# First FFN: the last two batches as tiles of chosen rows, two chains in the opening, and the choice of keys beside the tiles

## The reference, cut to what matters

```
x = x + haar_mixing(ln(x))     # q, v products, Haar transform, weights, inverse, W_out
x = x + ffn(ln(x))             # first FFN
x = x + sparse_attention(ln(x))# 16 heads: band of 128, 64 global keys, top 128 keys by a score
x = x + ffn(ln(x))             # second FFN, same weights

def ffn(x):                    # 8 experts, 128 -> 256 -> 128
    p = softmax(x @ Wg)
    w, i = top_k(p, 2);  w = w / (sum(w) + 1e-8)
    y[e] = square(relu(x @ W1[e])) @ W2[e]
    return sum over the two chosen e of w[e] * y[e]
```

## Time and profile before

| | |
|---|---|
| median of 3 runs | 570.01 us (569.81 to 571.88) |
| profiled execution, span | 568.3 us |
| PE busy | 517.5 us, 91% |
| DVE busy | 408.2 us, 72% |
| ACT busy | 350.6 us, 62% |
| POOL busy | 271.3 us, 48% |
| chain that ended last | PE 54%, DVE 30%, issue 8%, POOL 3%, ACT 3%, DMA 1% |

### The profile page before, as it was taken

One profiled execution on the slowest core, in us unless ns is written; L12 is line 12 of the kernel. 1 busy time (PEld: TensorE's weight loads), 2 busy tenths in 40 slices (PEclk: granted clock), 3 DMA queues, 4 the chain that ended last, 5 costly groups with the idle time before them and its releaser, 6 DMA issues.

```text
span 568.3 us, 13254 instructions
## 1 busy us (share of the span) xinstructions
PE 517.5 (91%) x4483; PEld 321.2 (57%) x4483; DVE 408.2 (72%) x1458; ACT 350.6 (62%) x775; POOL 271.3 (48%) x429
## 2 busy tenths in 40 slices
PE   5899999999996889988898999999998999889996
PEld 2467776767772445444544554555545553567875
DVE  2447575698999799999967878778688795134335
ACT  5476656656640266656774677676765657667763
POOL 2402030160605994674408985859916346264540
PEclk9999999999996899999999999999999999999999
DMA  7990000000000000000000000000100011575606
GB/s 228 336 273 2 0 2 1 0 2 1 11 2 13 2 15 12 8 12 16 12 14 4 15 13 13 6 20 30 34 5 13 17 42 43 196 258 173 206 19 186
DMA packets 33443, 31.99 MB, mean 56 GB/s; under 512 B 7250, under 2 KB 28502, under 8 KB 33376
## 3 DMA queue, kind: packets, MB, share of 16 engines
q1 hardware_dynamic: 31616, 27.80, 16.2%
q0 software_dynamic: 1760, 3.35, 1.7%
HBM read 8.57 MB, written 12.00 MB: 36 GB/s over the span
## 4 chain that ended last, share of the span: by engine, by line
PE 54%; DVE 30%; issue 8%; POOL 3%; ACT 3%; DMA 1%; SPq 0%; DVEq 0%; POOLq 0%; ACTq 0%
PE BANK L1565 6%; PE BANK L1547 6%; DVE QST L1221 5%; PE BANK L1615 4%; PE BANK L1665 4%; PE BANK L1640 3%; PE BANK L1668 3%; DVE SW L1175 3%; PE BANK L1501 2%; PE BANK L1511 2%; PE BANK L1671 2%; DVE X L1157 2%; DVE QST L1224 2%; DVE M L1173 2%; PE BANK L1526 2%
## 5 line engine op out<-in xcount | busy, mean ns | idle before, releaser
L819 ACT ACTIVATE PT<-BANK 128x256 f32<-128x256 f32 (+2 forms) x352 | 159.1, 492 | 98.0 <-PE BANK L1640 74.6
L553 POOL TENSOR_SCALAR OH<-IOTA,POS 128x128 bf16<-128x128 bf16 x240 | 139.8, 617 | 1.4 <-DVE POS L1189 1.0
L1216 DVE CUSTOM_DVE_ANT_0 XN_a<-BANK,BANDQ 128x256 f32<-128x256 f32 (+1 forms) x128 | 62.5, 488 | 22.9 <-PE BANK L1615 20.1
L1565 PEld LDWEIGHTS BANK<-W,PT 128*128 128x128 f32 x512 | 62.0, 192 | 15.2 <-issue 14.4
L1216 DVE CUSTOM_DVE_ANT_0 XN_c<-BANK,BANDQ 128x384 f32<-128x384 f32 (+1 forms) x128 | 62.3, 487 | 9.0 <-PE BANK L1615 7.4
L1565 PE MATMUL BANK<-W,PT 128*128 128x128 f32 x512 | 62.5, 275 | 0.0
L1547 PE MATMUL BANK<-XNT_ALL,W 128*128 128x512 f32 x128 | 60.6, 597 | 0.0
L730 ACT ACTIVATE PT<-BANK 128x512 f32<-128x512 f32 x64 | 38.0, 597 | 31.4 <-PE BANK L1547 30.9
L560 POOL TENSOR_TENSOR SUM<-NRM 128x128 f32<-128x128 f32 x16 | 7.3, 457 | 104.6 <-DVE NRM L1237 104.6
L1665 PE MATMUL BANK<-PT,V 128*32 128x256 f32 (+1 forms) x512 | 47.7, 444 | 1.9 <-ACT OS L828 0.4
L582 POOL DMA_INDIRECT yt<-QKV,IDY x31 | 30.4, 980 | 27.4 <-DVE QKV L1074 22.7
(11 more groups left out here) (300 smaller groups left out, 1185.2 us busy)
## 6 DMA issues: line engine op xcount, KB each, us to landing
xs<-W SPq DMA_DIRECT2D x1, 6984.0 KB, 27.5
KZB<-W SPq DMA_DIRECT2D x16, 256.0 KB, 2.4
KZC<-W SPq DMA_DIRECT2D x15, 256.0 KB, 2.6
QKV<-xs SPq DMA_DIRECT2D x31, 72.0 KB, 2.0
W<-w SPq DMA_DIRECT2D x2, 1024.0 KB, 8.1
X<-x SPq DMA_DIRECT2D x4, 256.0 KB, 3.2
out<-X SPq DMA_DIRECT2D x4, 256.0 KB, 2.2
KZB<-KALL SPq DMA_DIRECT2D x20, 36.0 KB, 1.9
```

The source lines that it names most:

```text
L553: last = nc.gpsimd.tensor_scalar(OH[g % 2][:, i, t, :], IOTA[:, :], POS[:, t, c:c + 1], None, ALU.is_equal)
L819: nc.scalar.activation(PT[u % PT_RING][:, 0:w], P2_BANK[u % SCORE_RING][:, 0:w], ACT.Exp, scale=SCALE).then_inc(S["exp_done"], 1)
L1216: nc.vector.tensor_tensor_reduce(out=JUNK[v % 2][:, 0:n], in0=P1_BANK[v % SCORE_RING][:, 0:n], in1=BANDQ[:, off:off + n], scale=1.0, scala ...
L1565: last = mm(DOWN_BANK[n % 2][:, t * P:(t + 1) * P], HID_T[n % 2][hh][:, t * P:(t + 1) * P], W2[:, e, hh, :], start=(hh == 0), stop=(hh == ...
```

## The change

The machinery of chosen rows is made general (a class `Wave` with its tags "early" and "late") and used a second time: in the first FFN batches 0 and 1 stay dense (16 pairs) and batches 2 and 3 become 23 tiles behind them.

```diff
+EARLY = Wave("early", 2, 2)
+LATE = Wave("late", 0, 3)
+PAIRS = EARLY.first * E
+NT_EARLY, NT = EARLY.nt, LATE.nt
...
-A_PERIOD = 5
-GATE_SPREAD = ((0, 1), (2, 3), (4, 5))
+A_PERIOD = 3
+GATE_SPREAD = ((0, 1, 2), (3, 4, 5))
...
+GATE_ONE = {1: (0, 1), 2: (2, 3), 3: (4, 5)}
+ROUTE_PAIR, SLOTS_PAIR = {9: 2, 12: 3}, {9: 2, 12: 3}
+TABLE_PAIR = {13: (0, 1), 14: (2,)}
+C_PAIR = 8
+C_TILE, SCORES_TILE, QK_TILE, P1_TILE = 2, 3, {5: 0, 6: 1}, 7
+ROUNDS_TILE = {i: 1 for i in range(4, NT_EARLY)}
+SPREAD_TILE = 11
```

The opening runs the chains of batches 0 and 1 in turns, with banks and buffers of their own for the second (`CHAIN`, `CHAIN_BANK`); only the last two steps of chain 1 lie beside the pairs. ScalarE scales q while it copies it, and DVE multiplies it by v straight from the bank:

```diff
+            for s in (1, 2):
+                a_step(s, 0)
+                a_step(s, 1)
...
+                    for lo, hi, w in BANDS:
+                        if w is None:
+                            nc.scalar.copy(dst[:, :, lo:hi], src[:, :, lo:hi]).then_inc(S["a_q_s"], 1)
+                        else:
+                            nc.scalar.activation(dst[:, :, lo:hi], src[:, :, lo:hi], ACT.Identity, scale=WPROD[:, w:w + 1],
+                                                 bias=BQV[:, 0:1] if w == 0 else 0.0)
```

TensorE behind the pairs:

```diff
+            for i in range(NT_EARLY):
+                tile_step(EARLY, i)
+                if i == C_TILE:
+                    c_turn(1)
+                if i == SCORES_TILE:
+                    pe.wait_ge(S["c_t_s"], PAIR)
+                    pe.wait_ge(R["early"]["idx"], EARLY.count)
+                    sel_scores(0)
...
+                if i == P1_TILE:
+                    pe.wait_ge(S["sel_score_s"], 1)
+                    pe.wait_ge(S["c_stored"], 2 * (T + 1))
+                for w in local_units(i):
+                    p1(0, w)
+            pe.wait_ge(R["early"]["tile_y"], NT_EARLY)
+            c_turn(2)
+            c_turn(3)
+            for t in range(T + 1):
+                c_qkv(2, t)
```

`local_units` spreads the first 20 score products of head group 0 over tiles 7 to 22. DVE, with half a round after each tile from tile 4 on:

```diff
+            for i in range(NT_EARLY):
+                tile_y(EARLY, i)
...
+                maxima(local_units(i))
+                rounds(0, ROUNDS_TILE.get(i, 0))
+            rounds(0, 3)
+            add_experts(EARLY, 2)
+            dve.wait_ge(S["x_sum"], 1)
+            stats("c", 2)
+            rounds(0, 2)
+            normalize("c", 2)
+            add_experts(EARLY, 3)
```

POOL and SP:

```diff
+            for b in range(2, B):
+                for n in range(2 * T):
+                    scatter(EARLY, b, n)
+            rstd("c", 1)
+            stacks(0)
+            for n in range(NT_EARLY):
+                tile_out(EARLY, n)
+                if n == 8:
+                    values(0)
+                if n == 16:
+                    stacks(1)
...
+                if n == SPREAD_TILE:
+                    sp.wait_ge(S["misc_free"], free("qk", 0) + 1)
+                    sp.wait_ge(S["heads_zero"], 3)
+                    spread(0, 0, KS0, KEYS_IN[0])
+                tile_load(EARLY, n, read[n % READ])
```

More of the change, by code:

```diff
@@ L145, with a_steps, local_units @@
 SEL_GROUP, SEL_AT, POS_AT = 5, 7, 11
[L148 to L152, removed]
+def a_steps(n):
+    if n < 2:
+        yield 5 + n, 1
+    for a in range(2, B):
+        step = n - A_PERIOD * (a - 2)
+        if 0 <= step < 7:
             yield step, a
+def local_units(i):
+    n, k = HG * (T + 1), NT_EARLY - P1_TILE
+    return range(n * max(i - P1_TILE, 0) // k, n * max(i - P1_TILE + 1, 0) // k)
 def shared_bank_uses():
@@ new lines, in results @@
+            def results(w):
+                for slot in range(Y_RING):
+                    sp.wait_ge(Y_OUT[w.tag][slot], 16 * slot_count(w, slot))
+                for b in range(w.count):
+                    for k in range(2):
+                        first = k * w.jt * P + b * L
+                        sp.dma_start(YB[w.tag][b][k], YT[w.tag][first:first + L, :].rearrange("(t p) d -> p t d", p=P)
+                                     ).then_inc(Y_IN[w.tag][b], 16)
+            sp.wait_ge(R["early"]["table"], 1)
@@ L802, in _ @@
+            c_turned(2)
+            c_turned(3)
             scores_out(1)
@@ L1094, in a_step @@
-                    last.then_inc(S["a_prod"], 1)
+                    dve.wait_ge(S["a_qv"], 2 * a + 2)
+                    dve.wait_ge(S["a_q_s"], a + 1)
+                    q, pr = (z[:, :].rearrange("p (t c) -> p t c", t=T) for z in (qs, pr))
+                    v = bank[2][:, :].rearrange("p (t c) -> p t c", t=T)
+                    hi = BANDS[0][1]
+                    nc.vector.scalar_tensor_tensor(out=pr[:, :, 0:hi], in0=v[:, :, 0:hi], scalar=BQV[:, 1:2],
+                                                   in1=q[:, :, 0:hi], op0=ALU.add, op1=ALU.mult)
@@ new lines, in _ @@
+            mask(0)
+            c_add(2, T)
+            c_add(3, 0)
+            c_add(3, 1)
+            dve.wait_ge(S["sel_t"], 1)
+            marks(BANK[4]).then_inc(S["sel_t_s"], 1)
+            c_add(3, 2)
+            c_add(3, 3)
+            dve.wait_ge(S["sel_pos"], 1)
+            places(0, BANK[5]).then_inc(S["sel_done"], 1)
+            dve.wait_ge(S["sel_done"], 1)
+            for i in range(HG):
+                for t in range(T):
+                    last = nc.vector.tensor_scalar(OH[0][:, i, t, :], IOTA[:, :], POS[:, t, i:i + 1], None, ALU.is_equal)
@@ L1317, in _ @@
+            last.then_inc(S["onehot_dve"], 1)
+            c_add(3, T)
+            gathered_kv(0)
+            maxima(range(HG * (T + 1), UNITS_Q))
             maxima(range(UNITS_Q, UNITS_Q + FIRST_LEAD))
@@ L1495, in tile_up, with tile_turn @@
-            def tile_up(n):
-                pe.wait_ge(S["tile_xt"], n + 1)
+                if b == w.first + w.count - 1:
+                    for j in range(w.jt):
+                        last = mm(bank[:, T * E:T * E + E], TRI[:, 1, :], MSK[:, j, :], start=(j == 0), stop=(j == w.jt - 1))
+                return last
+            def tile_turn(w, n):
+                r = R[w.tag]
+                pe.wait_ge(TILE_IN[w.tag][n % IN_RING], 32 * (n // IN_RING + 1))
+                if n:
+                    pe.wait_ge(r["tile_xt"], n)
+                nc.tensor.transpose(T_BANK[w.tag][:, 0:P], XT_IN[w.tag][n % IN_RING][:, 0:D], IDENT[:, :]).then_inc(r["tile_t"], 1)
```

1133 lines of the change are left out of this document (600 added, 533 removed).

## The result

| | before | after |
|---|---|---|
| median | 570.37 us (569.81 to 571.88, 4 runs) | 580.02 us (577.76 to 581.35, 4 runs) |
| ratio of the runs | | 1.016, 95% interval 1.0136 to 1.0185 |
| profiled execution, its span | 568.3 us | 579.4 us |
| PE, DVE, ACT, POOL busy | 517.5, 408.2, 350.6, 271.3 us | 493.1, 405.0, 335.5, 309.2 us |

The kernel got 9.7 us slower; 578.1 us was forecast. TensorE has 24.4 us less to do, and the time is longer all the same. The profiled execution of after itself took 581.17 us.

A forecast was written before the change was run, and what follows sets the result against it. TensorE was taken to bound the first FFN before. Terms 23.0 + 76.1 + 7.9 + 26.0 + 27.7 + 6.5 + 23.5 + 13.5 = 204.2 us start the loop, +8.1 on 570.0 gives 578.1 us; own range 573 to 583, given range 565 to 587.

The forecast's parts named there:

- Opening: Start up to the first dense pair: earlier than today's 27.26 us, at 23.0 us.
- Sixteen pairs: Dense pairs of the first FFN with TensorE's work beside them: 73.2 us counted plus 2.9, ending at 99.1 us.
- Gap: Between pairs and first tile: numbering, row sends and weights' load leave TensorE idle 8 us; first tile at 107.0 us.
- Tiles 0 to 8: First nine tiles: TensorE's work, pipe filling 2.5, late key spread 2, low clock 5; 26 us, to 133.0 us.
- POOL: After the ninth send: POOL's queue of sends, values and stacks sets the pace; last send begins at 160.7 us.
- Just inside: DVE in the tiles: at most 1.8 us a tile, through at 158.2 us, before POOL's last send at 160.7.
- Behind the last tile: Last send to the places: 6.5 us to the results, then 23.5, DVE's one unhidden line being 21.
- the forecast's bound of 1.7 us: Normalization behind POOL's values, after the last tile: port locking would lose it up to 1.7 us; 1.0 was added.
- From the places to the loop: One-hot, gather, spreads and maxima before the attention loop: 13.5 us instead of today's 22.7; loop starts at 204.2 us.
- Faster (565.8): Rival: tiles run at TensorE's pace, last send at 148.4 us, loop at 191.9, total 565.8 us; chance 0.20.
- Even (570): Rival: POOL's term holds, but opening, gap and clock cost 8 us less, total 570 us; chance 0.18.
- The clock low through half of the tiles and all of the tail (587): Rival: TensorE stays at 1.2 GHz there, +9 us, total 587 us; chance 0.10.

The follow-up runs named there:

- e0: The changed kernel again, unedited, as the measure for the experiments: 577.54 us against 569.71 us before, ratio 1.0145.
- e2: Changed kernel with the first key spread before tile 15's load instead of tile 11's, first scores behind tile 10 instead of 7: 600.52 us, ratio 1.0119, slower group.
- e3: Changed kernel with filler products on zeros in four TensorE waits (34, 42, 18, 12): 602.99 us, ratio 1.0177, slower group.
- e10: Changed kernel with slightly fewer filler products on zeros in the same four waits (32, 40, 17, 10): 601.83 us, ratio 1.018, slower group.
- the three others: Changed kernel with POOL's edit plus later key spread, fillers, and q, k, v of batches 2 and 3 behind the choice: 568.17 us, ratio 0.9973.
- e5: Changed kernel with ten of the thirteen half rounds behind the tiles moved beside the tiles: 577.76 us, ratio 1.0143.
- groups marked: Two of three groups of runs, where the kernel before took 592.1 and 591.8 us instead of 569.7; the unedited changed kernel has no run there.

## Why the prediction was right, and where it was not

The terms, read from the result's profile:

| step | predicted us | measured us |
|---|---|---|
| first pair | 23.0 | 24.87 (23.10 in e0) |
| 16 pairs, to their end | 76.1 | 74.3 |
| gap to the first tile | 7.9 | 8.2 |
| to the ninth send | 26.4 | 27.2 |
| to the last send | 27.3 | 28.5 |
| to the first sum | 6.5 | 6.1 |
| to the places | 23.5 | 23.0 |
| to the loop | 13.5 | 14.5 |
| loop starts at | 204.2 | 206.75 |
| from there on, with 1.7 to 1.8 outside the span | 373.9 | 374.4 |

*Opening.* Within 2 us; it varies by as much from one execution to the next of the same kernel.

*Sixteen pairs.* Too long by 1.8 us; an allowance of 2.9 us was added to the 73.2 counted. That this takes away the opening's 1.9 us is luck.

*Gap.* As counted: the last scatter began at 101.24 (100.8 forecast), the first turn at 107.38 (107.0). TensorE idle 8.22 us, the clock at 0.50 behind it.

*Tiles 0 to 8.* The length was right, in part by luck. The forecast put the spread's landing some 2 us late at tile 7, but not that tile 11's load stands behind it; e2 shows the whole at 2.0 us. For the clock 5 us were put down, and e3 and e10 won back 1.7 and 0.8 us. Against that, 2.5 us for filling the pipe was too little: the first send came 8.0 us behind the first tile, and 6.0 us in e3 and e10 with the clock at 1.00. What else makes up the stretch was not taken apart.

*POOL.* Right in mechanism: sends in three runs, DVE waiting for a landing (2.45 and 1.41 us), last send at 163.1 in the forecast 156 to 165. Without the block 24.2 us remain, at DVE's pace. "Just inside" was the right word for DVE, and it is why the edit gives 3.1 us (4.5 with the three others) and not the 9.4 of stacks and values.

*Behind the last tile.* Right in length, wrong in mechanism. The forecast said that DVE has one line of work here and "nothing hides it", and put 1.5 us on TensorE. e5 took 7.5 of the 21 us away and the stretch to the places fell from 22.7 to 21.3 us: there are two lines, DVE's, and one through POOL's factor and TensorE's products at half clock, of nearly one length. What was true is that nothing of either stood beside dense pairs any more. The second norm took 1.76 us beside POOL's values and the first 1.11 with POOL idle; 1.0 us was added, 0.65 lost. The Trainium skill (SBUF — State Buffer, "SBUF: two separate sides") has the two engines shut each other out for a whole instruction. The trace agrees in sign, and the forecast's bound of 1.7 us by that rule was not reached.

*From the places to the loop.* 1.0 us longer, with the clock at 0.50 from 198 us on; the four maxima of 2.49 us and the landing of the spread are as forecast.

*The rivals.* Faster (565.8): it put the last send at 148.4 us. Even the edit of POOL's queue leaves the pace to DVE; with SyncE's order and the fillers as well the last send comes at 153.0 us. Even (570): the opening, gap and clock did not cost 8 us less. The clock low through half of the tiles and all of the tail (587): it was low in a smaller part of the tiles (means of 0.81 and 0.86) and in most of the tail (0.61 and 0.63), but the work in the tail is 18 us only. The Trainium skill (TensorE: Matmul & The Clock Gate, "HAM oscillation — how this bites in real kernels") describes a kernel in which each wait for a DMA brings the clock down. In part the trace agrees: it fell around 132, 146 and 159 us and held 1.00 from 117 to 129 us through a wait of 0.51 us. The fillers that mended part of it gave 2.3 to 4.4 us in the stretches; what they give in the time the runs don't settle.

Open stays: what makes DVE and ScalarE stop in the groups marked *, and why the loop takes 20 us longer there; the time of the unedited kernel in these groups, and with it the single edits in us of the whole; whether the new opening with all four batches dense is better than either kernel.

## What to carry to other kernels

When bulk work is replaced by gathered work, count what had been hidden beside the bulk: here 56 us of dense pairs and what lay beside them went, a gap and tiles paced by a send queue took 64 us, and the tail behind lost its cover. Before shortening an engine's work in a tail, follow the second-longest line to the same end: 7.5 us of DVE's work gave 1.6. Look into each in-order queue for what stands between the pieces that pace the stage, and move it to where that queue is idle; and ask of a tail whether the consumer behind it needs its result at all: the loop needed only the choice, which could be made in the wait for the results.

## What the runs showed of the hardware

- Landing of a send (indirect, 128 rows): 2.1 to 4.1 us after the issue, median 2.3; the slowest, 4.07 us, held up DVE through the ring of four.
- Sixteen one-hots on DVE took 2.90 us beside POOL's own one-hots (the result's profile) and 4.54 us beside POOL's casts and subtractions (e7), 1.6 us more.
- All kernels ran about 4% slower in two of the three groups, almost all of it from the loop on (391 to 394 against 372 us), once under the same chip number as in the faster group. Waits without a releaser in the trace, up to 4.6 us, stood in every profile of the slower groups and in none of the others. A single edit and the kernel that it edits belong in one group; here they were not, and the single edits' worth stays known by stretches only.
